# Line ranks in a routed feed-forward kernel: sixteen shifted matmuls replaced by one scan on VectorE and one matmul

## The reference

```
x = x + conv_branch(layernorm_over_channels(x))     # two binarised 2x3 convolutions, batch norms, ReLUs
t = tokens(x)                                       # (16, 1024, 64)
n = layernorm(t)
logits = n @ gate_w + gate_b                        # 16 experts
top 2 of softmax(logits), weights renormalised      # dispatch
expert(e, n) = (silu(n @ w1[e]) * (n @ w2[e])) @ w3[e]
out = from_tokens(t + sum over the two experts of weight * expert(e, n))
```

## Time and profile before

| | |
|---|---|
| time, median of 3 runs | 535.71 us (534.81 to 540.6) |
| the profiled execution | 537.69 us, its span 536.0 us |
| TensorE (PE) busy | 474.1 us, 88% of the span, 4774 matmuls |
| VectorE (DVE) busy | 397.3 us, 74% |
| ScalarE (ACT) busy | 258.5 us, 48% |
| GpSimd (POOL) busy | 281.5 us, 53% |
| chain that ended last | PE 78%, DVE 9%, issue 4%, DMA 3%, ACT 3% |
| mean granted clock of TensorE | 0.932 of full speed |

### The profile page before, as it was taken

The page is one execution under the profiler, slowest core; times in us unless marked ns, Lnnn a source line. Parts: engine busy times, 40 slices in busy tenths (PEclk is TensorE's granted clock), DMA queues, the critical chain, the costliest instruction groups (busy, mean ns, idle before and its releaser), DMA issues.

```text
span 536.0 us, 15131 instructions
## 1 busy us (share of the span) xinstructions
PE 474.1 (88%) x4774; PEld 417.1 (78%) x4774; DVE 397.3 (74%) x913; ACT 258.5 (48%) x462; POOL 281.5 (53%) x378
## 2 busy tenths in 40 slices
PE   6889999899998245899999999999999999999991
PEld 5457676767776223899999999999999999999981
DVE  5547777888989988777777677777778777777772
ACT  4557778988777212343443434343433434334320
POOL 4000006777777777777776444444544445455552
PEclk9779879999989756899999999999999999999996
DMA  7981011122000014431233222232422525310234
GB/s 265 325 149 40 1 41 35 53 71 65 30 32 30 28 32 92 87 71 30 62 81 68 56 43 54 49 93 50 121 64 49 130 48 149 75 37 16 74 109 157
DMA packets 62664, 41.03 MB, mean 77 GB/s; under 512 B 50003, under 2 KB 54318, under 8 KB 62080
## 3 DMA queue, kind: packets, MB, share of 16 engines
q1 hardware_dynamic: 52208, 23.84, 19.9%
q0 software_dynamic: 8800, 8.94, 5.2%
q10 hardware_dynamic: 1584, 7.29, 3.4%
HBM read 21.46 MB, written 19.19 MB: 76 GB/s over the span
## 4 chain that ended last, share of the span: by engine, by line
PE 78%; DVE 9%; issue 4%; DMA 3%; ACT 3%; SPq 1%; POOL 0%; POOLq 0%; DVEq 0%; ACTq 0%
PE turn L943 27%; PE up L928 12%; PE up L929 12%; PE up L757 8%; PE small L773 4%; PE small L906 3%; PE small L802 3%; DMA x_in<-in_x 3%; PE up L732 2%; PE turn L785 2%; PE lines L829 1%; PE up L743 1%; PE turn L796 1%; PE lines L950 1%; ACT rstd_wide L576 1%
## 5 line engine op out<-in xcount | busy, mean ns | idle before, releaser
L519 POOL DMA_INDIRECT results<-result,page_in x147 | 145.2, 988 | 129.7 <-ACT xc L691 102.4
L498 POOL DMA_INDIRECT pages<-payload,slot_int x128 | 130.4, 1018 | 108.6 <-DVE slot_int L1351 70.2
L691 ACT ACTIVATE xc<-up,gate_unscale 128x512 f32<-128x512 f32 x147 | 101.1, 687 | 175.5 <-PE up L929 143.6
L928 PE MATMUL up<-xs_hi,up_w 128*128 128x128 f16 x1176 | 148.7, 220 | 3.5 <-DVE hidden L1523 2.0
L929 PE MATMUL up<-xs_lo,up_w 128*128 128x128 f16 x1176 | 148.7, 220 | 0.0
L928 PEld LDWEIGHTS up<-xs_hi,up_w 128*128 x1176 | 123.4, 105 | 4.7 <-issue 4.0
L929 PEld LDWEIGHTS up<-xs_lo,up_w 128*128 x1176 | 115.7, 98 | 0.0
L1523 DVE SCALAR_TENSOR_TENSOR hidden<-up,hidden_scale,xc 128x512 f32<-128x512 f32 x74 | 55.4, 750 | 41.0 <-ACT xc L691 41.0
L943 PE MATMUL turn<-down_raw,hidden 128*128 x592 | 77.7, 275 | 3.4 <-issue 1.7
L943 PE MATMUL turn<-down_raw,sq 128*128 x584 | 78.1, 277 | 2.5 <-issue 0.7
L943 PEld LDWEIGHTS turn<-down_raw,sq 128*128 128x128 f32 x584 | 70.8, 191 | 10.3 <-issue 7.9
(11 more groups left out here) (234 smaller groups left out, 618.2 us busy)
## 6 DMA issues: line engine op xcount, KB each, us to landing
pages<-x ACTq DMA_DIRECT2D x4, 1332.0 KB, 10.8
page_in<-pages SPq DMA_DIRECT2D x147, 36.0 KB
page_in<-pages SPq DMA_DIRECT2D x147, 32.0 KB
x_in<-in_x SPq DMA_DIRECT2D x7, 512.0 KB, 3.5
out<-up_raw SPq DMA_DIRECT2D x5, 512.0 KB, 3.1
results<-result,page_in POOLq DMA_INDIRECT x147
up_raw<-in_L_ffn_w SPq DMA_DIRECT2D x4, 512.0 KB, 17.6
pages<-payload,slot_int POOLq DMA_INDIRECT x128
```

The costliest lines, as they stand in the source:

```text
L498: pool.indirect_dma_start(out=pages, out_offset=bass.IndirectOffsetOnAxis(ap=slot_int[q % PAYLOADS][:, t:t + 1], axis=0), in_=payload[q % ...
L519: pool.indirect_dma_start(out=results, out_offset=bass.IndirectOffsetOnAxis(ap=page_in[g % LOADS][:, k, D + AT_TOKEN:D + AT_TOKEN + 1].bit ...
L691: act.activation(act_s[n % 2], up[n % 2][:, 0:CW], ACT.Silu, scale=gate_unscale[:, 0:1])\
L928: pe.matmul(target, own, xs_hi[g % 2][:, at], start=True, stop=False)
```

## The change

The marks are laid out line by line (20 lines of 17 tiles, `hot`), and `line_hot` becomes a view of them in which neighbouring lines lie 17 elements (34 bytes) apart. On VectorE, `line_parts` begins with one scan over 339 marks: `hot_before[i+1] = same_line[i] * hot_before[i] + hot[i]`, where `same_line` is 0 at each line's 17th place, so that the sum starts afresh on each line. `hot_before` then holds, for each line and tile, the marks of the preceding tiles on the same partition. `rank` keeps its first two matmuls, and a third one, of ones with `hot_before` in a strided view (340 columns), replaces the sixteen. TensorE waits for the scan (`before_ready`) ahead of that third matmul. Three memsets and one wait are added to the tables that VectorE makes at the start.

```diff
-        line_hot = sb("line_hot", [P, TILES + 1, LINES], BF16)
+        hot = sb("hot", [P, LINES * (TILES + 1)], BF16)
+        hot_before = sb("hot_before", [P, LINES * (TILES + 1)], BF16)
+        same_line = sb("same_line", [P, LINES * (TILES + 1)], BF16)
+        line_hot = hot[:, :].rearrange("p (l t) -> p t l", l=LINES)
...
                 pe.matmul(rank_ps, upper_b[:, :], line_hot[:, :, :], start=True, stop=False, skip_group_check=True)
                 pe.matmul(rank_ps, ident_b[:, :], left_b[:, :].unsqueeze(1).to_broadcast([P, TILES + 1, LINES]),
                           start=False, stop=False, skip_group_check=True)
-                for s in range(1, TILES + 1):
-                    last = pe.matmul(rank_ps[:, s:TILES + 1, :], ones_b[:, :], line_hot[:, 0:TILES + 1 - s, :],
-                                     start=False, stop=(s == TILES), skip_group_check=True)
-                last.then_inc(ranks_ready, 1)
+                pe.wait_ge(before_ready, q + 2)
+                pe.matmul(rank_ps, ones_b[:, :], hot_before[:, :].rearrange("p (l t) -> p t l", l=LINES),
+                          start=False, stop=True, skip_group_check=True).then_inc(ranks_ready, 1)
...
                 dve.memset(line_hot[:, TILES:TILES + 1, :], 0.0)
+                dve.memset(hot_before[:, 0:1], 0.0)
+                dve.memset(same_line[:, :], 1.0).then_inc(before_ready, 1)
+                dve.wait_ge(before_ready, 1)
+                dve.memset(same_line[:, :].rearrange("p (l t) -> p t l", l=LINES)[:, TILES:TILES + 1, :], 0.0)
...
             def line_parts(q):
                 rows = payload[q % PAYLOADS]
                 dve.wait_ge(hot_ready, q + 1)
+                dve.tensor_tensor_scan(out=hot_before[:, 1:], data0=same_line[:, :-1], data1=hot[:, :-1],
+                                       initial=0.0, op0=ALU.mult, op1=ALU.add).then_inc(before_ready, 1)
                 then(dve.tensor_reduce(upright[:, :], line_hot[:, 0:TILES, 16:LINES], AX.X, ALU.max))
```

More of the change, by code:

```diff
@@ L286, in metaformer_kernel @@
         gap_ready, gap_done = sem("gap_ready"), sem("gap_done")
+        before_ready = sem("before_ready")
         chosen_ready, chosen_turned, chosen_read = sem("chosen_ready"), sem("chosen_turned"), sem("chosen_read")
```

## The result

| | before | after |
|---|---|---|
| time, median of 4 runs | 538.15 us (534.81 to 542.61) | 556.0 us (550.21 to 562.65) |
| the profiled execution, span | 537.69, 536.0 us | 550.21, 548.5 us |
| mean granted clock of TensorE | 0.932 | 0.907 |

The changed kernel is slower: 1.0251 times the time before, 95% interval 1.0192 to 1.0311, some 13.5 us.

A forecast was written before the change was run, and what follows sets the result against it. The prediction took waits for ScalarE's squares and VectorE to limit gains from the rank's 7.0 us on the chain. Gains of -2.25 and the scan's +1.82 sum to -0.43, giving 535.3 us from the 535.71 median; range 531.4 to 539.6.

The forecast's parts named there:

- The layout: Marks written and read 34 bytes apart by `find_line`, `slots` and two rank matmuls: 0 for VectorE and for TensorE.
- The forecast's upper bound, 0.32 us for 320: Most the stride could cost a VectorE operation on 320 marks: one more 1.01 ns per element.
- Twice 0.14: Doubled price assumed for each strided rank matmul; pair 2's rank would still end before ScalarE's squares, so 0.
- the gains at pairs 2 and 3: TensorE's variance starting sooner behind the shorter rank: -0.27 us at pair 2, -0.63 at pair 3.
- the 1.35 forecast as gain: At pair 0, the variance starts at 76.07 instead of 77.42, right behind ScalarE's squares: -1.35 us.
- the marks' stride slows VectorE: Rival: `find_line` in eight pairs and `slots` in pairs 4 to 7 lose 0.32 us each, 539.2 us; chance 0.10.
- the clock falls more often: Rival: TensorE, now waiting for the squares, loses clock, 1.3 to 1.6 us a fall, 536.6 to 539.5; chance 0.17.
- the signs that the prediction named against itself: Scan beyond 1.2 us, marks' write or `slots` product beyond 0.55, or granted clock near 0.5 around pair 1's or 2's rank.
- The scan: VectorE's scan of 339 elements: 0.91 us, hidden in pairs 0 to 4, adding 1.82 us over pairs 5 and 6.
- In pair 7: Roster ends at 211.00, replacing the 0.92 us wait of `rows_low` for ScalarE: 0.
- The net of the working, -0.43 us: Sum over the kernel: TensorE's gains of -2.25 us plus the scan's +1.82.

The follow-up runs named there:

- e3: Kernel before, with 26 unused operations added at the start that write, read and multiply 320 elements at several strides; only the single operations' times are given.
- e4: Changed kernel with marks, counts, ranks and products all laid out line by line, only the last sum of `slots` strided: 548.34 us, ratio 1.0192.
- e5: e4 plus fifteen matmuls with zeros between the second and third matmul of the rank: 542.39 us, ratio 1.0071.
- e12: Kernel before, with `find_line` first writing the same 320 marks twice to spare tiles nobody reads: 545.89 us, ratio 1.0145.
- e2: Changed kernel, with `find_line` writing the marks adjacently in memory order and reading PSUM 80 bytes apart: 547.15 us, ratio 1.0176.
- e1: Kernel before, layout and sixteen matmuls kept, plus the scan with an unused result and TensorE's wait for it: 542.9 us, ratio 1.0076.
- e11: e4 with e8's filler matmuls and more behind its ranks, 21 for pairs 0 and 1, then 6: 532.12 us, ratio 0.9905.
- e10: Kernel before with e8's filler matmuls and 3 to 12 more at the end of steps 1 to 7: 530.61 us, ratio 0.9895.
- e8: Kernel before with unused matmuls, eight ahead of `norm` in steps 1 to 7, 44 and 40 in the last two steps: 539.06 us, ratio 0.9882.

## Why the prediction was wrong

**The step that failed is "The layout", taken as 0 for VectorE and for TensorE.**
- *The write.* It was priced from a write of 16 elements of 32 bits 288 bytes apart, which took as long as an adjacent one. e3 shows why that row could not tell. For 320 f32 elements a wide stride costs 0.12 us, 6 ns for 16 of them; for bf16 it costs 0.53, again only 26 ns for 16. The row had another type and too few elements. The forecast's upper bound, 0.32 us for 320, was no bound: the change lost 1.01. (In e3, reading from SBUF, the same stride cost 0.53; why `find_line`, which reads from PSUM, pays twice that was not tried.)
- *The matmuls.* "Twice 0.14" was a guess with no row behind it; it is 0.57 to 0.60. Where the clock was up, the three so take as long as the eighteen (1.45 and 1.46 us at pair 2), the variance waits for L833 and not for ScalarE, and the gains at pairs 2 and 3 could not arrive. At pair 0 the variance does wait for the squares (0.55 us), as forecast, but the convolution behind it then lost 1.46 us, more than the 1.35 forecast as gain.
- *The rival that named it* (the marks' stride slows VectorE) had mechanism and sign right, and a third of the write's size: 8.1 us for eight, where it had 0.32 each. For the product of `slots` its 0.32 was near the 0.23 measured.

**The clock was the second miss.** The rival "the clock falls more often" gave 1.3 to 1.6 us for a fall. In the changed kernel it fell behind pairs 0, 3 and 4, and the convolution alone lost 1.5, 1.6 and 2.2 us. The rival said itself that TensorE would wait for the squares where it had worked; the sum booked that wait as free. e4 and e5 show that it is not: with adjacent marks the kernel lost 1.9%, and useless work in the place of the work removed gave two thirds of that back. Had the layout been right, the forecast would have failed by this.

In the changed kernel itself that wait stood behind pair 0's rank alone. Behind pairs 3 and 4 the variance followed L833 at once, and the rival's cause was missing. What differed from before was the longer wait ahead of `norm` (1.86 us for 0.91) and the strided matmuls. e12 has a longer wait too (1.70 us at pair 0, 1.71 at pair 2), and its convolutions stay quick; e2 has the strided matmuls with the old wait (0.91 at pairs 2 and 3), and there the clock falls. That points to the strided matmuls. It isn't shown, since no run changes them alone, and behind pairs 1 and 2 of the changed kernel the same matmuls left the convolution quick.

Of the signs that the prediction named against itself, three came: the write and the product beyond 0.55 us, and a clock of 0.50 around pair 1's rank.

**The scan was right in size and nearly in place.** Forecast 0.91 us, measured 0.856. That it came so near is in part luck: what was added for the scan hung on a difference of 0.024 us, and the row of the scan of 20 alone varies by 0.012. It lies on the path in pairs 5 and 6, as said, and nowhere in pairs 0 to 4 (e1). In pair 7 the profile after has `rows_low` (L1459) straight behind the roster, as forecast:

```profile
222.71 0.17 DVE roster L1453
222.88 0.59 DVE xs_lo L1459
```

The 0.92 us of waiting that the earlier trace rows show there are gone; the scan and the longer write together needed 1.9. The page that bears on the size (the Trainium skill, DVE: opcode table, instruction layouts, handler registers and perf-mode slots, section "Datapath and trigger behaviour") says that this scan runs at half throughput; 0.856 for 339 elements against 0.484 for 320 is 1.77 times as long. Without the 0.16 us that the rows leave for an operation of no elements (0.176 for 16, 1.01 ns each) it is 2.05 ns an element against 1.01, which agrees.

**The net of the working, -0.43 us, was found in no run.** The nearest is e11 against e10, adjacent marks and a clock held by fillers: 532.1 and 530.6 us, 0.3% apart and the other way.

Of the loss of 2.5%, the runs thus show 0.8% for the scan and its wait (e1) and 1.4%, by an interval from 0.4 to 2.5%, for a `find_line` longer by about as much (e12). The rest, and how far the slow write hid falls of the clock that e2 then showed, can't be split: the causes are not additive.

## What to carry to other kernels

Before changing a layout, price the new stride with the same type and as many elements as the kernel's own, on every engine that touches it; a row with 16 elements can't show a cost per element. When work goes from TensorE and it then waits for something else, look at the granted clock in the stretch behind the wait: the removed work may have been what held it, and strided matmuls in its place may not hold it though the engine is busy. Where waits can't be shortened, matmuls that compute nothing, put into them, can be worth a per cent (e10, 0.9895); with fewer of them (e8) it came in four executions of ten.

## What the runs showed of the hardware

- TensorE reading bf16 columns 16 bytes or more apart takes 0.57 us for 320 columns, at a granted clock of 1.00 as at 0.50; adjacent ones take 0.14 at 1.00.
- Busy without a pause in such matmuls, TensorE's granted clock fell from 1.00 to 0.50 (e3); behind two of them and one adjacent one it did the same (e2, pair 2).
- From SBUF, VectorE writes 320 bf16 elements in 0.33, 0.35, 0.53, 0.88 us at 2, 4, 8, 16 bytes; f32 elements lose only 0.12 at 64 (e3). From PSUM, bf16 at 34 bytes takes 1.49 for 0.48; reading PSUM 80 bytes apart and writing adjacent elements takes 0.485 (e2).
- The kernel before itself stands at two places by its clock: of the seven runs beside e12, three lie at 535.0 to 535.7 us (granted 0.935 to 0.938), three at 541.6 to 541.8 (0.927) and one at 545.0 (0.921).
